# Logits and second norm two chunks later, run ends filled from SBUF two per chunk, eight experts' split weights kept over the dense blocks

## The reference

```python
# x: 10000 x 128, adj: 10000 x 10000, all float32
h = item_feat @ W_item.T + b_item
b = layernorm(x) @ W_user.T + b_user
x = x + relu(adj @ h + b)                       # stage 1: one pass over 400 MB of adj
z = layernorm(x)                                # second norm
probs = softmax(z @ gate_w + gate_b)            # 8 experts, the two largest are kept with their probs
for e in range(8):                              # expert: 128 -> 256 -> 128
    x = x + cw[:, e:e+1] * (gelu(z @ W1[e] + b1[e]) @ W2[e] + b2[e])
```

## Time and profile before

| | us |
|---|---|
| median of 3 runs | 1561.77 (1561.69 to 1563.81) |
| the profiled execution, total | 1562.79 |
| its span, first to last instruction | 1561.0 |
| PE busy | 1476.0 (95%) |
| DVE busy | 1278.2 (82%) |
| ACT busy | 1103.5 (71%) |
| POOL busy | 807.3 (52%) |
| moved by DMA | 502.29 MB, mean 322 GB/s |

### The profile page before, as it was taken

The page is one execution under the profiler, slowest core; times in us unless marked ns, Lnnn a source line. Parts: engine busy times, 40 slices in busy tenths (PEclk is TensorE's granted clock), DMA queues, the critical chain, the costliest instruction groups (busy, mean ns, idle before and its releaser), DMA issues.

```text
span 1561.0 us, 20673 instructions
## 1 busy us (share of the span) xinstructions
PE 1476.0 (95%) x6682; PEld 1181.8 (76%) x6682; DVE 1278.2 (82%) x1677; ACT 1103.5 (71%) x1178; POOL 807.3 (52%) x596
## 2 busy tenths in 40 slices
PE   8999999999999999999996899999999989999887
PEld 6787787787787877877875688888888877777555
DVE  5778788788788887887885788888888978788898
ACT  4666767667677677677673778797878768787655
POOL 0114534634635544446344178776877865676420
PEclk9999999999999999999998899999999999999999
DMA  9889999999999999999996998989898888786675
GB/s 356 298 315 337 351 371 345 354 365 335 369 346 340 375 343 343 382 331 355 364 331 227 348 329 320 334 331 333 322 332 326 324 306 304 273 280 226 215 237 195
DMA packets 144649, 502.29 MB, mean 322 GB/s; under 512 B 35696, under 2 KB 41792, under 8 KB 144286
## 3 DMA queue, kind: packets, MB, share of 16 engines
q1 hardware_dynamic: 127518, 479.25, 84.1%
q0 software_dynamic: 17024, 21.73, 4.1%
HBM read 468.77 MB, written 36.31 MB: 324 GB/s over the span
## 4 chain that ended last, share of the span: by engine, by line
PE 57%; DVE 15%; POOL 13%; issue 7%; ACT 3%; DMA 3%; SPq 2%; DVEq 0%; ACTq 0%; POOLq 0%
PE p_agg L502 16%; PE p_agg L497 14%; PE p_agg L498 14%; DVE s_a_lo L952 6%; POOL s_rs L1315 3%; POOL rr L1353 2%; POOL s_rs L1327 2%; PE p_hid L479 2%; DVE s_h_hi L1178 1%; POOL s_rs L1316 1%; ACT s_a_hi L743 1%; DMA s_raw<-adj 1%; POOL s_rs L1319 1%; PE p_agg L513 1%; PE p_hid L590 1%
## 5 line engine op out<-in xcount | busy, mean ns | idle before, releaser
L952 DVE TENSOR_TENSOR s_a_lo<-s_raw,s_a_hi 128x1500 fp32r<-128x1500 f32 x520 | 885.6, 1717 | 144.7 <-PE p_agg L502 92.4
L743 ACT ACTIVATE s_a_hi<-s_raw 128x1500 fp32r<-128x1500 f32 x520 | 751.0, 1454 | 220.2 <-PE p_agg L502 183.1
L497 PE MATMUL p_agg<-s_a_hi,s_h_hi 128*128 128x500 f32 x1560 | 635.4, 407 | 22.7 <-ACT s_a_hi L743 22.7
L498 PE MATMUL p_agg<-s_a_hi,s_h_lo 128*128 128x500 f32 x1560 | 615.1, 394 | 0.0
L502 PE MATMUL p_agg<-s_a_lo,s_h_hi 128*128 128x500 f32 x1560 | 450.8, 398 | 33.4 <-DVE s_a_lo L952 31.8
L1344 POOL DMA_INDIRECT zs<-s_rows,s_idx x136 | 225.6, 1659 | 309.2 <-DVE s_idx L1080 215.3
L502 PEld LDWEIGHTS p_agg<-s_a_lo,s_h_hi 128*128 128x128 f32 x1560 | 293.9, 191 | 115.1 <-DVE s_a_lo L952 56.6
L497 PEld LDWEIGHTS p_agg<-s_a_hi,s_h_hi 128*128 128x128 f32 x1560 | 299.4, 192 | 87.6 <-ACT s_a_hi L743 29.4
L498 PEld LDWEIGHTS p_agg<-s_a_hi,s_h_lo 128*128 128x128 f32 x1560 | 299.8, 192 | 58.1 <-issue 3.2
L1353 POOL DMA_INDIRECT rr<-s_ysb,s_dests x192 | 271.7, 1415 | 136.7 <-DVE s_ysb L1163 84.4
L1335 POOL TENSOR_TENSOR s_gt<-s_ebase,s_gt 125x32 f32<-125x32 f32 x20 | 129.9, 6495 | 48.3 <-DVE s_gt L1006 48.1
(11 more groups left out here) (215 smaller groups left out, 1433.2 us busy)
## 6 DMA issues: line engine op xcount, KB each, us to landing
s_raw<-adj SPq DMA_DIRECT2D x520, 750.0 KB, 6.7
s_wraw<-w SPq DMA_DIRECT2D x72, 256.0 KB, 4.1
s_zt<-zs SPq DMA_DIRECT2D x48, 264.0 KB, 3.1
s_raw<-rr SPq DMA_DIRECT2D x34, 256.0 KB, 3.8
s_xtok<-x_tok SPq DMA_DIRECT2D x20, 256.0 KB, 6.8
s_xt<-x_t SPq DMA_DIRECT2D x20, 250.0 KB, 7.1
out_s<-s_x1s SPq DMA_DIRECT2D x17, 256.0 KB, 6.9
s_raw<-out_s SPq DMA_DIRECT2D x17, 256.0 KB, 3.3
```

The lines of the kernel that those rows point to most:

```text
L497: mm(o, h_hi[:, k * D:(k + 1) * D], hi, start=(k == 0), stop=False)
L498: mm(o, h_lo[:, k * D:(k + 1) * D], hi, start=False, stop=False)
L743: fn(a_hi[:, n % HIS, :], raw[:, n % RAW, :], ACT.Copy).then_inc(hi_made, 1)
L952: tt(a_lo[:, n % LOS, :], raw[:, n % RAW, :], a_hi[:, n % HIS, :].bitcast(F32), ALU.subtract)\
```

## The change

1. `logits` goes from chunk 9 to 11, with POOL's `power` (same constant); `ln2_norm` from 10 to 12; the first norm (`LN1_AT`) from 13 to 15; softmax, both choices, prefix, the turn and copy of the first norm, slots (and with them the scatter) and the table one chunk later each.
2. The eight fills of a group are issued two at each of four chunks (6 to 9 of the block) instead of eight at chunk 5, with SBUF as source. The source tile no longer shares `ysb` but lies in `early`, which grows to 528 columns and is set by POOL at n = 52; the table's scratch `big` moves to `gt`. The first tile's loads come at chunk 10, `FIRST_W1` goes from chunk 10 to 14 of its block, and `STEP` of the second group falls from 2.35 to 2.12 (tiles at 482, 484, ... 498, 501, ... 515).
3. In the dense part the weights are loaded, rounded and split for the first eight items only and stay: experts 0 to 2 in `wt`, 3 to 7 in `h_lo`. The biases of all experts come by one more DMA near the start (`dbias`), 1024 runs of 12 bytes.

```diff
-X1_AT, X1T_AT, BN2_AT, BN1_AT, X1S_AT, LG_AT, LN2_AT = 1, 1, 4, 5, 4, 9, 10
-TAILHI_AT, TAILLO_AT, SOFT_AT, TOP1_AT, TOP2_AT, LN1_AT = 9, 10, 15, 16, 17, 13
-PREFIX_AT, LN1T_AT, SLOT_AT, LN1C_AT = 18, 16, 20, 19
-TABLE_AT = (20, 21, 22)
+X1_AT, X1T_AT, BN2_AT, BN1_AT, X1S_AT, LG_AT, LN2_AT = 1, 1, 4, 5, 4, 11, 12
+TAILHI_AT, TAILLO_AT, SOFT_AT, TOP1_AT, TOP2_AT, LN1_AT = 9, 10, 16, 17, 18, 15
+PREFIX_AT, LN1T_AT, SLOT_AT, LN1C_AT = 19, 17, 21, 20
+TABLE_AT = (21, 22, 23)
...
-FILL_AT = [(hi + 1) * CH + 5 for lo, hi in GROUPS]
-FIRST_W1 = [(hi + 1) * CH + 10 for lo, hi in GROUPS]
+FILL_AT = [(hi + 1) * CH + 6 for lo, hi in GROUPS]
+FIRST_W1 = [at + E // 2 + 4 for at in FILL_AT]
...
-ZT_LOAD = [0, 0] + [max(W1_AT[k - 2] + 3, FILL_AT[k >= NTG[0]] + 1) for k in range(2, NT)]
+ZT_LOAD = [0, 0] + [max(W1_AT[k - 2] + 3, FILL_AT[k >= NTG[0]] + E // 2) for k in range(2, NT)]
...
+        dbias = sb("dbias", [P, E, 3])
...
-        early = sb("early", [P, 3 * D])
+        early = sb("early", [P, SUBS * W])
...
-            i = (o - NT) % 6
-            if o >= NT and i >= 3:
-                w0 = 12 * UB + (i - 3) * 4 * HID + lo * 2 * HID
-                return h_hi[:, w0:w0 + 2 * HID]
+            e = (o - NT) % E
+            if o >= NT and e >= 3:
+                w0 = (e - 3) * 4 * HID + lo * 2 * HID
+                return h_lo[:, w0:w0 + 2 * HID]
+            if o >= NT:
+                return wt[:, e, lo, :]
...
-            def fill_ends(g):
-                sp.wait_ge(scattered, 2 * 16 * SUBS * GROUPS[g][1])
-                sp.wait_ge(tab_made, 2 * (g + 1))
-                sp.wait_ge(spare_filled, 16 * 2)
-                for e in range(E):
-                    r = sp.value_load(fillat[0:1, g, e:e + 1], min_val=0, max_val=SPARE0[g] - T)
-                    sp.dma_start(zs[bass.ds(r, T), :].rearrange("(p s) w -> p (s w)", s=SUBS),
-                                 zs[SPARE0[g]:SPARE0[g] + T, :].rearrange("(p s) w -> p (s w)", s=SUBS))\
-                        .then_inc(filled, 16)
+            def fill_end(g, e):
+                if e == 0:
+                    sp.wait_ge(scattered, 2 * 16 * SUBS * GROUPS[g][1])
+                    sp.wait_ge(tab_made, 2 * (g + 1))
+                r = sp.value_load(fillat[0:1, g, e:e + 1], min_val=0, max_val=SPARE0[g] - T)
+                sp.dma_start(zs[bass.ds(r, T), :].rearrange("(p s) w -> p (s w)", s=SUBS),
+                             fill.rearrange("p s w -> p (s w)")).then_inc(filled, 16)
...
+                    sp.dma_start(dbias[:, :, :], b12.rearrange("e p n -> p e n")).then_inc(late_loaded, 16)
...
-                    if n == FILL_AT[g_]:
-                        fill_ends(g_)
-                if n == FILL_AT[0] + 1:
+                    if 0 <= n - FILL_AT[g_] < E // 2:
+                        fill_end(g_, 2 * (n - FILL_AT[g_]))
+                        fill_end(g_, 2 * (n - FILL_AT[g_]) + 1)
+                if n == FILL_AT[0] + E // 2:
...
-                if j + 4 < ND:
+                if j + 4 < E:
                     load_w(NT + j + 4)
...
-                if d >= 0 and d + 2 < ND:
+                if 0 <= d and d + 2 < E:
                     w_rest(NT + d + 2)
```

More of the change, by code:

```diff
@@ L159, in build @@
         ints = sb("ints", [1, NTHR + NTG[0] + E * E])
-        fill = ysb[:, :, :].rearrange("p a n -> p (a n)")[:, 0:SUBS * W].rearrange("p (s w) -> p s w", w=W)
+        fill = early[:, :].rearrange("p (s w) -> p s w", w=W)
         bn = sb("bn", [P, 2 * SUBS, 6])
@@ L177, in build @@
         tbl = sb("tbl", [1, 4, NTG[0]])
-        big = early[0:1, 0:NTG[0] * E]
         tab = sb("tab", [1, 2, NT], I32)
         fillat = sb("fillat", [1, 2, E], I32)
+        big = gt[0:1, :, :].rearrange("p a n -> p (a n)")[:, 0:NTG[0] * E]
         lg, zz, ez, pr, kk, pr2, slot, msk = (gt[:, i, :].rearrange("p (s e) -> p s e", e=E) for i in range(8))
@@ L204, in build @@
         b2_hi, b2_lo, b2_split = sem("b2_hi"), sem("b2_lo"), sem("b2_split")
-        gsum_done, gatec_made, base_set, spare_set, spare_filled = (
-            sem("gsum_done"), sem("gatec_made"), sem("base_set"), sem("spare_set"), sem("spare_filled"))
+        gsum_done, gatec_made, base_set, spare_set, spare_filled, fill_set = (
+            sem("gsum_done"), sem("gatec_made"), sem("base_set"), sem("spare_set"), sem("spare_filled"),
+            sem("fill_set"))
         tail_hi, tail_split = sem("tail_hi"), sem("tail_split")
@@ L283, in comb, with parts_made @@
             return flat[:, c0:c0 + T]
-        def tiles_to(o):
-            return min(o, NT)
+        def parts_made(o):
+            return min(o, NT + E - 1) + 1
         block = ctx.enter_context(nc.Block())
@@ L327, in load_w @@
                     sp.wait_ge(h_prod, CH + 1)
-                if o >= 4:
+                if 4 <= o < NT:
                     sp.wait_ge(gelu_done, o - 3)
-                    sp.wait_ge(yt_made, tiles_to(o - 3))
-                e = sp.value_load(tab[0:1, 1, o:o + 1], min_val=0, max_val=E - 1) if o < NT else (o - NT) % E
+                    sp.wait_ge(yt_made, o - 3)
+                e = sp.value_load(tab[0:1, 1, o:o + 1], min_val=0, max_val=E - 1) if o < NT else o - NT
                 sp.dma_start(wraw[:, o % 2, :], w12[bass.ds(e, 1)].rearrange("a p n -> (a p) n"))\
                     .then_inc(w_loaded[o % 2], 16)
-                sp.dma_start(bias[:, o % 4, :], b12[bass.ds(e, 1)].rearrange("a p n -> (a p) n"))\
-                    .then_inc(w_loaded[o % 2], 16)
+                if o < NT:
+                    sp.dma_start(bias[:, o % 4, :], b12[bass.ds(e, 1)].rearrange("a p n -> (a p) n"))\
+                        .then_inc(w_loaded[o % 2], 16)
             def load_zt(k):
@@ L417, in _ @@
                 if n == 3 * CH + 3:
-                    sp.wait_ge(spare_set, 4)
+                    sp.wait_ge(fill_set, 2)
                     for g_ in range(2):
@@ L584, in first_layer @@
             def first_layer(o, n, hi, lo):
-                pe.wait_ge(w_split, o + 1)
+                pe.wait_ge(w_split, parts_made(o))
                 for h in range(2):
@@ L784, in ln2_norm @@
                 if p == 0:
-                    act.wait_ge(sets, 5)
+                    act.wait_ge(sets, 4)
                 r = rows[0] if p < S else rows[(p - S) % 2]
@@ L804, in w_round @@
             def w_round(o):
-                act.wait_ge(w_loaded[o % 2], 32 * (o // 2 + 1))
-                before = wpart_before(o)
-                if NT + 3 <= o < NT + 6:
+                late = max(o - NT + 2, 0) // 2
+                act.wait_ge(w_loaded[o % 2], 32 * (o // 2 + 1) - 16 * late)
+                if o >= NT + 3:
                     act.wait_ge(chunk_used, NCH)
-                elif before >= 0:
-                    act.wait_ge(w2_done, before + 1)
+                elif o >= 3:
+                    act.wait_ge(w2_done, o - 2)
                 fn(wpart(o, 0), wraw[:, o % 2, :], ACT.Copy).then_inc(w_hi, 1)
@@ L852, in dense_gelu @@
                 if d == 0:
+                    act.wait_ge(late_loaded, 16 * NL)
                     act.wait_ge(lo_made, NCH)
@@ L856, in dense_gelu @@
                 for h in range(2):
-                    fn(dg(d)[:, h * UB:(h + 1) * UB], hid[h][:, 0:UB], ACT.Gelu, bias=bias[:, o % 4, h:h + 1])\
+                    fn(dg(d)[:, h * UB:(h + 1) * UB], hid[h][:, 0:UB], ACT.Gelu, bias=dbias[:, d % E, h:h + 1])\
                         .then_inc((gelu_half, gelu_done)[h], 1)
@@ L1363, in _ @@
             gp.memset(rows[1][:, :, :], 0.0).then_inc(sets, 1)
-            gp.memset(ysb[:, :, :], 0.0).then_inc(sets, 1)
-            pool.wait_ge(sets, 5)
+            pool.wait_ge(sets, 4)
             pool.wait_ge(late_loaded, 16 * NL)
-            gp.tensor_scalar(fill[:, :, D + 1], dest0[:, :], float(DUMP + 2 * T), None, ALU.add).then_inc(spare_set, 1)
             for i in range(2):
@@ L1372, in _ @@
             rstd(0)
-            pool.wait_ge(spare_set, 4)
+            pool.wait_ge(spare_set, 3)
             for n in range(LAST):
@@ L1383, in _ @@
                         scatter(p)
+                if n == 2 * CH:
+                    pool.wait_ge(h_prod, CH + 1)
+                    pool.wait_ge(gsum_done, 1)
+                    pool.wait_ge(bb_split, 1)
+                    gp.memset(fill, 0.0).then_inc(fill_set, 1)
+                    pool.wait_ge(fill_set, 1)
+                    gp.tensor_scalar(fill[:, :, D + 1], dest0[:, :], float(DUMP + 2 * T), None, ALU.add)\
+                        .then_inc(fill_set, 1)
                 for k in range(NT):
```

10 lines of the change are left out of this document (3 added, 7 removed).

## The result

The changed kernel takes 1538.2 us (median of 6, 1535.3 to 1546.1), the kernel before 1562.5 in the same comparison: ratio 0.985, 95% interval 0.984 to 0.987. The kernel is 24 us faster. Forecast were 61 and 1501 us, with 1484 to 1524 as the range. The time is outside it, and the gain is 0.4 of what was forecast.

The account below looks back on a forecast made before the run. PE was taken as the bound, stalled in blocks 1 to 12 and at fills, with DVE binding dense items that combine. Terms −46 − 6 − 4.5 − 6.4 + 1 + 1 = −60.9 gave 1501 us, range 1484 to 1524.

Parts of the forecast that it names:

- A: Blocks 1 to 12: logits two chunks later remove DVE's wait for `rs` and PE's stall; −46 us, ends −50 and −33.
- the stall comes back: Rival, blocks 1 to 12: DVE early or scatter delaying `rs`, PE idles again; half of the logits' gain, 1524 us; chance 0.08.
- DVE's wait for `rs` in front of the logits is gone: Sign for blocks 1 to 12: the wait, up to 3.3 us in each block, would vanish.
- the clock of 1.00 and the 699 us: Signs for blocks 1 to 12: TensorE at clock 1.00 and the stretch taking about 699 us.
- What I gave back to the DMA: Blocks 1 to 12: 4 us of the logits' 50 us gain given back for late loads here and there.
- the rival at 366 GB/s: Rival: DMA becomes the bound, blocks 1 to 12 take 708 us, total 1514 us; chance 0.22.
- B: Group one's fills: issued in pairs, PE's first idle goes from 14.9 to about 7.2 us; −6, ends −14 and −1.
- C: Group two's fills: no scatter wait, SP's lead covers the pairs, 6 us lost become 1.5; −4.5, ends 0 and −6.
- E: Group two's closer tiles: `ysb` stalls +2 to +4, tile-turn stalls −3; +1 us, ends −3 and +7.
- POOL as the bound of the second group: Rival: a tile's sends need over 8.5 us, every tile makes PE wait for `ysb`; 1576 us, chance 0.02.
- D: Dense part: sixteen DVE splits go, items with combining reach PE's 3.68 us; −6.4 us, ends −4 and −9.6.
- F: Start: the added bias DMA stands ahead of later loads on SP's queue, 0.45 to 5 us; taken as +1.

Follow-up runs that it names:

- e3: Changed kernel with the first three of POOL's eleven operations for `rs` done by DVE behind its statistics; 1515.0 us, ratio 0.969.
- e9: Kernel of e3 with POOL, in block 13 alone, sending the first sparse tile ahead of the scatter; 1507.1 us, ratio 0.965.
- e4: Changed kernel with DVE making `a_lo` for only half of a chunk's columns from block 1 on, leaving out part of the result; 1475.0 us, one run.
- e8_no_moves: Changed kernel with the old chunk numbers of logits to table, so only fills, tiles and dense part changed; 1540.4 us.
- e5_again: Changed kernel run once more, unaltered, for a second profile (the "second execution"); 1537.4 us.
- e7: Changed kernel with POOL sending sparse tiles ahead of the scatter wherever both fall on one chunk; 1538.2 us.
- e6: Kernel before the change with only the kept weights of the dense part and the added bias load; 1558.9 us, ratio 0.997.
- e11: Kernel of e10_plus_lg12 with SP's first two weight loads ahead of group one's fills and the second tile's load one chunk later; 1517.9 us.
- e1: Changed kernel with logits at chunk 13 instead of 11, second norm at 14, first norm and softmax to table one chunk later; 1523.6 us, ratio 0.975.
- e10_plus_lg12: Kernel of e9 with the logits at chunk 12 and the second norm at 13; 1517.8 us.

## Why the forecast was wrong, part by part

**A, the logits, is the whole miss.** Forecast −46. Blocks 1 to 12 gave −9, and +5.5 in block 14 was the price of the moved scatter beside the first tiles' sends. The step that failed is "`rs` is made in one run of POOL from 232.52 to 242.65; nothing in the change moves this run". I took the run's 10.1 us for a duration, when it was 4 us of work and 6 of waiting for DVE, and the change alters what DVE does in that time: the run became 13.5 us. It could be seen: the earlier trace rows have an operation of 125x8 with 3.23 us and one with 0.20. I took the spread for POOL's own, though the run in block 13, with DVE idle, lasted 4.01. The rival "the stall comes back" asked for a DVE that is early or a scatter that is late; its price was worked out for half of A at 0.08, and the mechanism was neither. "DVE's wait for `rs` in front of the logits is gone" was the first sign named, and it did not come; nor did the clock of 1.00 and the 699 us for the twelve blocks (0.99 and 725).

With the stall really away (e3, e9) a block takes 58.4 us, not the 57.0 that 50 us less in twelve blocks meant. e4, where DVE has time to spare, shows 56.7, so the idea of what a block could be was right, and what is left is DVE itself. In e9 the clock is 1.00, and the 1.7 us lie in two places of a block: in block 4 chunks 12 and 13, behind the logits, take 0.8 us more than in e4, and 18 and 19, behind softmax and the choices, 0.9 more. PE's own waits for `a_lo` there are 0.3 us once in a block and 0.9 once in all.

**What I gave back to the DMA (4 us) and the rival at 366 GB/s (chance 0.22)** were wrong: 377 GB/s stood for 693 us with a DMA share of 0.99 and PE never idle. "348 GB/s at 0.95 busy are 366 at full" takes the busy share for a measure of room, which it isn't: 369 to 377 GB/s all come with 0.99 (e9, e4). The Trainium skill (page "DMA: Bandwidth & Descriptors", section Specifications) gives some 358 GB/s as a core's share of device memory; here, with one core at work, e4 went above it for 693 us.

**B, fills of group one.** Forecast −6, with the first idle at 7.2; block 13 gave −6.5 and −10.0 in the two executions and −11.0 in e8_no_moves. PE's chunk in front of the new load took 9.6 and 6.9 us (2.04 of it work), so the first idle was 7.4 us in one execution and 4.7 in the other. The second chunk of 8.1 and 5.7 us, behind the last pair, was in the sum as a second idle of 3.2. The steps held. Of the sizes, the issue of a pair of fills from SBUF occupies SP for some 1.5 us, not 2.6; but a pair with its load still came only every 3.2 to 3.8 us, against the 3.1 of the sum.

```profile
839.67 1.49 SPq L383 DMA_DIRECT2D zs<-s_early  x2
841.51 1.16 SPq L297 DMA_DIRECT2D s_raw<-adj  x1
843.45 1.46 SPq L383 DMA_DIRECT2D zs<-s_early  x2
```

**C and E, group two.** Forecast −4.5 and +1; blocks 18 and 19 gave −7.0 and −7.7, with fills all but hidden (3.8 us for the chunk that took 7.8 before). The premise of C, no wait for scatters in front of these fills, held narrowly: SP waited 1.9 us in e5_again, 10.3 in e7. Of E's terms, PE's stalls at the turn of a tile fell from 3.7 to 0.8 us as worked out, and those for `ysb` from 1.3 to 0.8 instead of rising by 2 to 4. What E missed is block 14: I looked at the second group's tiles only, though `FIRST_W1` moved the first group's too, by four chunks, onto the scatter. +5.5 us, shown by e7 and e8. POOL as the bound of the second group (0.02) did not come.

**D, dense part.** Forecast −6.4; −6.0 in the second execution against before, −4.8 in e6. Items with combining take 3.68 us, as worked out. Right.

**F, the start.** Forecast +1. The table counts from the first chunk; from the span's start, block 1 begins at 97.5 us before and at 98.4 in the second execution, so +0.9, and in nine other profiles with this DMA at 97.7 to 98.2. In the first execution and in e11 it begins at 100.4 and 100.1; whether the added DMA has a part in that is open. The DMA behind the 1024 short runs held SP for 2.8 to 3.6 us in the twelve profiles with it, beside 0.33 before, which is the mechanism that I feared, but most of the time the loads had the lead to cover it:

```profile
8.82 0.49 SPq L402 DMA_DIRECT2D s_dbias<-b  x1
9.35 3.33 SPq L403 DMA_DIRECT2D s_yt<-tri  x1
```

The sum without A was forecast as −14.9; e8_no_moves, which is that sum, gave −22. So the parts beside A did better than forecast, A gave 2 to 3 of 46.

## What to carry to other kernels

Before a wait is moved out of the way of a producer, ask whether the producer runs at its own speed: if operations of one shape have two durations in the trace, lay the other engine's rows beside them. If the long ones end with that engine's operations, the wait that you mean to remove may be what lets the producer finish, and two chunks of distance buy little. Here fewer operations on the held engine took the wait away (e3), and so did four chunks of distance (e1), which made the scatter late. And a shift by one chunk is to be checked against every queue that it passes: here it put a scatter in front of the first tiles' sends (5.5 us), and undoing that everywhere cost as much in another block.

## What the runs showed of the hardware

**POOL doesn't begin an operation beside DVE's subtraction of two SBUF operands.** POOL's operations of 0.20 us, issued during such an operation (1.72 us), ended 0.06 to 0.08 us behind it in block 3 of the changed kernel; eleven of them took 4.0 us with DVE idle, 5.5 beside DVE operations of 0.94 us, and 10.1 or 13.5 beside those of 1.72. The Trainium skill (page "SBUF — State Buffer", section "Who interferes with whom") has this rule: a DVE instruction with two SBUF inputs contends with a GpSimd instruction that reads SBUF, and the one issued second is blocked fully. This trace agrees for POOL as the second. It agrees on the two SBUF inputs too: in block 14 of e5_again POOL's operation at 937.59 took its 0.20 us within DVE's subtraction of 937.36 to 938.04, of which one operand lies in PSUM.

The wait is at the beginning alone. In block 3 of e1_lg13 DVE didn't stop behind the subtraction that held POOL's power operation of 125x8:

```profile
236.33 3.15 POOL L1329 TENSOR_TENSOR s_rs<-s_rs,s_consts 125x8 f32<-125x8 f32 x1
236.22 3.36 DVE L956 TENSOR_TENSOR s_a_lo<-s_raw,s_a_hi 128x1500 fp32r<-128x1500 f32 x2
```

DVE's first subtraction ends at about 237.9 and the power operation at 239.48, so its 1.55 us of work, as much as with DVE idle (1.54), ran beside the second. Nor do these runs show the reverse, a subtraction that POOL holds: POOL's power operation of 125x32, on record from 241.87 for 6.84 us in e10_plus_lg12, held none of the `a_lo` operations beside it, which take 1.72 us as ever:

```profile
241.71 1.72 DVE L956 TENSOR_TENSOR s_a_lo<-s_raw,s_a_hi 128x1500 fp32r<-128x1500 f32 x1
244.17 3.35 DVE L956 TENSOR_TENSOR s_a_lo<-s_raw,s_a_hi 128x1500 fp32r<-128x1500 f32 x2 [0.75 <-ACT s_a_hi L746]
```

Counted from the end of the first of them (243.43), the power operation took 5.28 us with two more subtractions beside it. In block 14 of the same run it took 5.33 us from the end of a subtraction with DVE idle. Why POOL's longer work isn't disturbed, no run shows.

**A DMA with 1024 runs of 12 bytes delays the next issue on its queue**, not its own: 0.4 to 0.5 us for itself, 2.8 to 3.6 us for the one behind it (0.33 without it).
